# Sorted rows of a mixture's half loaded from DRAM in one transfer in place of four

## The reference

```python
x = x + _L0_xattn_ref(_layernorm(x), ctx_1024, ...)   # 8 heads
x = x + _L0_ffn_ref(_layernorm(x), ...)               # f0: 8 experts, top 2, and a shared one; gelu
x = x + _L1_xattn_ref(_layernorm(x), ctx_1024, ...)   # 8 wide heads with position scores
x = x + _L1_ffn_ref(_layernorm(x), ...)               # f1: top 2, silu, with an inner layer
x = x + _L2_xattn_ref(_layernorm(x), ctx_1024, ...)   # 16 heads
x = x + _L2_ffn_ref(_layernorm(x), ...)               # f2: top 2, relu
x = x + _L3_xattn_ref(_layernorm(x), ctx_1024, ...)   # 16 heads
x = x + _L3_ffn_ref(_layernorm(x), ...)               # f3: top 1, gelu
```

## Time and profile before

| | us |
|---|---|
| median of 3 runs | 806.21 |
| lowest and highest | 806.12, 817.81 |
| the profiled execution | 808.12 |
| its span | 806.4 |
| PE busy in it | 634.6 (79%) |
| DVE, ACT, POOL busy | 415.5, 373.7, 184.8 |
| mean granted clock of PE | 0.887 of full speed |

### The profile page before, as it was taken

The page is one execution under the profiler, slowest core; times in us unless marked ns, Lnnn a source line. Parts: engine busy times, 40 slices in busy tenths (PEclk is TensorE's granted clock), DMA queues, the critical chain, the costliest instruction groups (busy, mean ns, idle before and its releaser), DMA issues.

```text
span 806.4 us, 14301 instructions
## 1 busy us (share of the span) xinstructions
PE 634.6 (79%) x4784; PEld 486.8 (60%) x4784; DVE 415.5 (52%) x1410; ACT 373.7 (46%) x930; POOL 184.8 (23%) x352
## 2 busy tenths in 40 slices
PE   4398659998898988687756589987997469978790
PEld 2165459886665666586755347755996324546790
DVE  6675533524266678656123567772544277873320
ACT  7065225554464546764443146653332126755460
POOL 1234313030040010413120411132313051131111
PEclk8599679999999999989797679997998759998996
DMA  5894089110677771201491313324174413431211
GB/s 155 252 358 158 13 166 189 33 37 27 163 244 217 230 213 53 76 14 50 148 144 53 75 43 73 112 90 89 54 202 79 102 31 85 154 102 43 76 50 49
DMA packets 92978, 90.76 MB, mean 113 GB/s; under 512 B 10980, under 2 KB 83301, under 8 KB 92716
## 3 DMA queue, kind: packets, MB, share of 16 engines
q1 hardware_dynamic: 89324, 82.51, 38.0%
q0 software_dynamic: 3584, 7.35, 3.6%
HBM read 53.06 MB, written 35.59 MB: 110 GB/s over the span
## 4 chain that ended last, share of the span: by engine, by line
PE 48%; DVE 15%; DMA 12%; POOL 9%; issue 8%; ACT 5%; SPq 1%; DVEq 0%; POOLq 0%; ACTq 0%
PE bank L1854 10%; PE bank L1875 9%; PE bank L1696 4%; PE bank L1644 3%; DMA late<-rows_sorted,idx 3%; PE bank L1679 3%; POOL rows_sorted L621 3%; PE bank L1983 2%; PE bank L1790 2%; DMA rows_sorted<-stage 2%; DVE negmax L878 2%; PE bank L1950 2%; POOL xm L631 2%; PE bank L1831 1%; POOL late L631 1%
## 5 line engine op out<-in xcount | busy, mean ns | idle before, releaser
L1875 PE MATMUL bank<-W,spare 128*128 128x128 f32 (+1 forms) x960 | 132.9, 284 | 1.4 <-ACT spare L1447 0.9
L1875 PEld LDWEIGHTS bank<-W,spare 128*128 128x128 f32 x960 | 122.8, 200 | 3.2 <-issue 2.1
L878 DVE TENSOR_REDUCE negmax<-bank 128x2 f32<-128x512 f32 x128 | 85.3, 689 | 48.7 <-PE bank L1644 32.0
L1644 PE MATMUL bank<-big 128*128 128x256 bf16 x320 | 73.3, 306 | 36.7 <-DMA big<-parts_scratch 26.0
L1363 ACT ACTIVATE late<-bank 128x512 f32<-128x512 f32 x120 | 70.8, 595 | 56.6 <-PE bank L1684 26.9
L1447 ACT ACTIVATE spare<-bank,W 128x128 f32<-128x128 f32 x224 | 64.0, 372 | 41.5 <-PE bank L1854 41.5
L621 POOL DMA_INDIRECT rows_sorted<-xn,idx x56 | 55.6, 992 | 109.2 <-DVE idx L955 94.6
L1679 PE MATMUL bank<-big 128*128 128x256 bf16 x320 | 74.6, 284 | 2.6 <-ACT late L1363 1.2
L1644 PEld LDWEIGHTS bank<-big 128*128 128x128 bf16 x320 | 28.6, 105 | 65.8 <-issue 36.7
L1495 ACT ACTIVATE big<-big,r 128x256 f32<-128x256 f32 x64 | 31.9, 500 | 45.8 <-DVE r L1189 45.7
L1696 PE MATMUL bank<-late 128*32 128x256 f32 x480 | 44.7, 399 | 0.1
(11 more groups left out here) (280 smaller groups left out, 1372.6 us busy)
## 6 DMA issues: line engine op xcount, KB each, us to landing
W<-in_f_wx SPq DMA_DIRECT2D x25, 578.0 KB, 7.2
late<-bands_scratch SPq DMA_DIRECT2D x8, 1024.0 KB, 5.5
W<-in_f_wx SPq DMA_DIRECT2D x8, 514.0 KB, 3.5
bands_scratch<-zrow SPq DMA_DIRECT2D x4, 768.0 KB, 12.7
big<-parts_scratch SPq DMA_DIRECT2D x6, 512.0 KB, 5.5
stage<-rows_sorted SPq DMA_DIRECT2D x11, 256.0 KB, 3.3
rows_sorted<-stage SPq DMA_DIRECT2D x11, 256.0 KB, 3.3
parts_scratch<-big SPq DMA_DIRECT2D x3, 768.0 KB
```

The source lines that it names most:

```text
L878: ins = v.tensor_reduce(negmax[:, g % 2, :, j], bank[i % 2][:, :].rearrange("p (t k) -> p t k", t=2), AX.X, ALU.max, negate=True)
L1644: ins = mm(o, Qs[:, h, S * b + 128 * t:S * b + 128 * (t + 1)], Ks[:, h, S * b:S * (b + 1)], start=True, stop=not mask)
L1875: ins = mm(dst[:, 128 * place_:128 * (place_ + 1)], hidB[n % 3][:, c, :], w2[:, 128 * c:128 * (c + 1)], start=c == 0, stop=c == FC - 1)
```

## The change

`rows_in` issues one transfer for all blocks of a half, of 128 partitions x 15 blocks x 128 values (11 in f3), and counts it on one semaphore per half. PE waits for that semaphore before every quad's transposes; the count is reached once for the half, so the waits for the later quads are met already. The `y_out` transfers stay one per quad. The diff:

```diff
-        def received(key, hf, q):
-            return sem(f"got{hf}.{q}"), quad_count(key, q)
+        def received(key, hf):
+            return sem(f"got{hf}"), 16 * (MIXTURES.index(key) + 1)
...
                 sp.wait_ge(sem(f"sent{hf}"), sent_total(key))
-                for q in range(quads[key]):
-                    n = quad_blocks(key, q)
-                    sp.dma_start(got(key, hf)[:, 512 * q:512 * q + 128 * n].rearrange("p (e c) -> p e c", c=D),
-                                 rows_sorted[hf][512 * q:512 * q + 128 * n, :].rearrange("(e r) c -> r e c", r=128))\
-                      .then_inc(received(key, hf, q)[0], 16)
+                n = sorted_blocks[key]
+                sp.dma_start(got(key, hf)[:, 0:128 * n].rearrange("p (e c) -> p e c", c=D),
+                             rows_sorted[hf][0:128 * n, :].rearrange("(e r) c -> r e c", r=128))\
+                  .then_inc(received(key, hf)[0], 16)
...
-                    pe.wait_ge(*received(key, hf, q))
+                    pe.wait_ge(*received(key, hf))
```

## The result

The changed kernel took 819.5 us in the median (816.8 to 820.4) against 806.2 before: a ratio of 1.018, 95% interval 1.012 to 1.024. Forecast was 818.7. In time that is 13.3 us; the profiled executions are 820.4 and 808.1 us, 12.3 apart.

The account below looks back on a forecast made before the run. PE was taken to set the time wherever it has data, waiting only for each half's first quad. Later landings summed to 12.5 us on the profiled 808.1, so 820.6; less 1.9 for timed runs, 818.7, range 810 to 826.

Parts of the forecast that it names:

- L: Time from a half's single issue to the landing of its rows: 5.2 us for 960 KB, 4.5 for 704 KB.
- f0.0: First half of mixture f0: rows land after 5.9 us, where the first quad took 2.9; cost +3.0 us.
- f1.0: First half of mixture f1: landing 2.4 us later, 1.5 absorbed by PE's idle time; cost +0.9 us.
- f1.1: Second half of mixture f1: PE had already idled 7.47 us for the landing; cost +2.7 us.
- f2.0: First half of mixture f2: landing after 7.4 us, with line 399's zeros in the rows' way; cost +4.5 us.
- f3.0: First half of mixture f3: PE's own work hides the landing, 732.6 against transposes at 733.49; cost 0.
- f3.1: Second half of mixture f3: landing later by 4.5 - 3.1, on the chain with PE idle; cost +1.4 us.
- f0.1: Second half of mixture f0: transfers issued while PE has most of the first half's blocks before it; cost 0.
- f2.1: Second half of mixture f2: PE's work hides the landing thinly, each 0.1 us over 5.6 costing 0.1; cost 0.
- Rival A: Staggered issue was the cost: one transfer could land in 3.6 to 4.5 us; 811.4 us at 4.3; chance 0.15.
- Rival B: 512-byte pieces make one long transfer slow: landing up to 8.3 us, two hidden halves exposed, 833.5 us; chance 0.15.
- Rival C: PE's low clock after stalls comes back, returning up to 13.8 us: 806.2 us or just under; chance 0.05.

## Why the prediction was right

Step by step, the forecast against the first profile of the changed kernel:

| half | L forecast | L measured | cost forecast | idle time grown by |
|---|---|---|---|---|
| f0.0 | 5.9 | 5.8 | 3.0 | 2.8 |
| f1.0 | 5.2 | 5.6 | 0.9 | 2.4, less 1.5 absorbed = 0.9 |
| f1.1 | 5.2 | 5.5 | 2.7 | 2.9 |
| f2.0 | 7.4 | 6.8 | 4.5 | 3.8 |
| f3.0 | 4.5 | 4.8 | 0 | 0.3 |
| f3.1 | 4.5 | 4.9 | 1.4 | 1.9 |
| f0.1, f2.1 | 5.2 | 5.6, 5.5 | 0 | 0 |
| sum | | | 12.5 | 12.6 |

- **That only the first quad is waited for** held: giving it a transfer of its own brings the time back to that of before, and putting it last among four costs what the change does.
- **L** from the 1024 KB load and from the four loads of f1.1 was 0.3 to 0.4 us short. Crowding was real in f2.0; taking the zeros away gave 5.4. But its size, 4.5 forecast against 3.8, was a guess between bounds 3.4 us apart, and with the zeros behind them the rows landed after 6.4, 6.8 and 8.0 us in three profiles. In f0.0, 5.6 to 5.8 us against 5.3 to 5.7 elsewhere is all that could be crowding, and no run tested it. That the sum fits to 0.1 us is luck: f0.0 and f2.0 were put 0.9 us too high, and f1.1, f3.0 and f3.1 1.0 too low.
- **The absorbed 1.5 us in f1.0** are gone from the list of waits, as forecast.
- **Rival A** (3.6 to 4.5) fell with the landings, and with the reversed order. The Trainium skill's formula (page "DMA: Bandwidth & Descriptors", section Anatomy of one DMA) gives, as an estimate, 3.2 us for 512 KB and 4.25 for 960; the section fits it to transfers issued from GpSimd, and these are issued from SP. The runs show 4.1 to 4.4 and, where no zeros stand behind, 5.3 to 5.7 on the quicker chips. The same page's advice to coalesce (Rules for kernel authors) is for many small transfers, and puts those under 64 KB down as mostly overhead; these were of 256 KB, and merging them gained nothing here (1.000 with 14 fewer).
- **Rival B** (past 6 us) did not come about: f2.1 kept its cover at 5.5 against 5.6 needed.
- **Rival C** (the clock comes back) did not come about: from 563 to 572 us, behind f2.0, it was at 0.50 as in the earlier trace rows. But the stretches at low clock did change their length, which the forecast names as a sign of being wrong. By the times of the same matmuls, those behind f1.1 and f2.0 gave back 0.9 us each, and those behind f0.0 and f3.1 cost 0.7 more each, together 0.4 us of gain. The forecast counts no such term; that it came to so little is chance as far as the runs show.
- What the forecast did not see is that the size of the cost belongs to the chip as well. Its "nothing in the kernel runs to a date of its own" does not hold on the slower chip, where PE came later to f1.0 and f2.0 and most of their landing was covered. On the third chip the changed kernel cost 10 us (ratio 1.007 to 1.017); the forecast 12.5 (1.015) lies in that interval, and the 13.3 of the first comparison is at its upper end.

## What to carry to other kernels

A transfer that one consumer uses piece by piece costs what its first piece waits. Merging the pieces behind the first was free here; let the first go alone and in front. Before moving a transfer look at what the waiting engine has queued behind the wait: 16 ready matmuls moved ahead of it in two places gained 3.4 us in the median, and 14 transfers removed gained nothing.

## What the runs showed of the hardware

- Loads of 512-byte rows from DRAM to 128 partitions landed after 2.5 to 3.1 us (256 KB, alone or first of several), 4.1 to 4.4 (512 KB), 4.7 to 5.0 (704 KB) and 5.3 to 5.7 (960 KB), on the quicker chips and where nothing crowded them. On the slower chip 960 KB took 5.6 to 6.1 us in f0.1, f1.0 and f1.1, and 6.9 and 7.2 in f2.1.
- A transfer issued behind another can slow it: zeros over 12 partitions lifted a 960 KB load from 5.4 to 6.4, 6.8 and 8.0 us in three profiles on such chips.
- Two chips differ in the same kernel by 30 us (809 and 839), with ACT and DVE waiting on the slower one for something outside the trace.
- The same stretch ran at a granted clock of 0.50 in one profile of the kernel before and at 1.00 in another. Such a swing was worth 4 us there and some 6 in the attention before f3, a third to a half of the effect measured here.
